# Row maxima turned by one product and a small DMA; half of head 1's mask moved from TensorE to VectorE

## The reference: two layers of attention, each with a feed-forward block behind it

```python
x = x + xattn0(layernorm(x), ctx, mask)       # 16 heads of 16; masked scores are -inf
x = x + moe_capacity(layernorm(x))            # top-2 of 8 experts, with a capacity
x = x + xattn1(layernorm(x), ctx, attn_mask)  # the same, but a float [512, 1024] mask is added to the scores
x = x + moe_top2(layernorm(x))                # top-2 of 8 experts
# attention: softmax over the 1024 keys of (q k^T / 4 + mask), times v, then a projection
```

## Time and profile before

| | |
|---|---|
| three runs | 1136.79, 1134.47, 1134.74 us; median 1134.74 |
| the profiled execution's own time | 1133.98 us |
| its span, first to last instruction | 1132.3 us |
| busy: TensorE, VectorE, ScalarE, GpSimd | 95%, 48%, 44%, 43% of the span |
| DMA | 170.52 MB, mean 151 GB/s |

### The profile page before, as it was taken

How to read it: one execution, slowest core, us unless ns; L and a number is a source line. 1 busy time by engine, 2 the same in 40 slices (tenths; PEclk the granted TensorE clock), 3 DMA queues, 4 the chain that set the end, 5 groups by cost and what they waited for, 6 DMA issues and landing times. The chain is left out here.

```text
span 1132.3 us, 25620 instructions
## 1 busy us (share of the span) xinstructions
PE 1078.0 (95%) x10259; PEld 770.2 (68%) x10259; DVE 547.0 (48%) x1534; ACT 493.4 (44%) x738; POOL 488.4 (43%) x510
## 2 busy tenths in 40 slices
PE   7899999999899999999899999999994999999997
PEld 4555655654578888888664344444454999999997
DVE  4579888864821111111347887777455122111221
ACT  4467777776531111111042788888853111111110
POOL 4457888883066892000004444444503223333232
PEclk8999999999999999999979999999998999999999
DMA  8744222002547964453079322210006999899970
GB/s 217 170 103 91 44 44 45 2 2 85 206 148 204 328 211 149 148 185 94 9 241 228 65 45 49 56 28 2 3 22 194 384 375 347 306 321 313 311 249 2
DMA packets 89632, 170.52 MB, mean 151 GB/s; under 512 B 11058, under 2 KB 61444, under 8 KB 87092
## 3 DMA queue, kind: packets, MB, share of 16 engines
q1 hardware_dynamic: 80916, 157.33, 44.4%
q0 software_dynamic: 6048, 8.28, 3.0%
q10 hardware_dynamic: 2560, 3.41, 1.1%
HBM read 150.19 MB, written 19.54 MB: 150 GB/s over the span
## 5 line engine op out<-in xcount | busy, mean ns | idle before, releaser
L189 PE MATMUL s_ps<-k_stack,q_stack 97*32 97x512 bf16 x1904 | 211.4, 382 | 2.8 <-ACT q_stack L281 2.3
L1488 ACT ACTIVATE prob<-st_ps 128x1024 f32<-128x1024 f32 x186 | 189.6, 1022 | 49.2 <-PE st_ps L189 44.8
L189 PE MATMUL st_ps<-q_stack,k_stack 100*32 100x512 bf16 x2048 | 193.2, 379 | 2.0 <-ACTq L1458 0.9
L252 DVE CUSTOM_DVE_ANT_0 junk<-s_ps,bias_rows,mx 128x512 f32<-128x512 f32 x240 | 170.1, 748 | 32.4 <-PE s_ps L189 32.4
L252 DVE CUSTOM_DVE_ANT_0 junk<-s_ps,bias_rows 128x512 f32<-128x512 f32 x236 | 154.6, 689 | 43.8 <-PE s_ps L189 43.7
L1935 PE MATMUL h_ps<-expert_in,w 128*128 (+1 forms) x704 | 153.5, 379 | 1.3 <-DMA w<-in_w 0.7
L1375 PE MATMUL o_ps<-prob,v_unit 128*32 128x512 f32 x1024 | 142.8, 595 | 4.3 <-POOL prob L1287 1.6
L1935 PEld LDWEIGHTS h_ps<-expert_in,w 128*128 128x128 f32 (+1 forms) x704 | 131.4, 187 | 22.0 <-issue 2.0
L1287 POOL TENSOR_TENSOR prob<-prob,keep_cols 128x1024 int32<-128x1024 int32 x56 | 132.9, 2383 | 21.4 <-ACT prob L1488 21.0
L2370 ACT ACTIVATE silu<-gu_ps 128x512 f32<-128x512 f32 x46 | 27.5, 597 | 227.3 <-PE gu_ps L2307 227.3
L189 PEld LDWEIGHTS st_ps<-q_stack,k_stack 100*32 100x32 bf16 x2048 | 72.6, 97 | 73.7 <-issue 21.0
(11 more groups left out here) (360 smaller groups left out, 1504.4 us busy)
## 6 DMA issues: line engine op xcount, KB each, us to landing
wg<-in_gateT SPq DMA_DIRECT2D x23, 1024.0 KB
wu<-in_upT SPq DMA_DIRECT2D x23, 1024.0 KB
wd<-in_downT SPq DMA_DIRECT2D x23, 1024.0 KB
w<-in_w SPq DMA_DIRECT2D x16, 1368.0 KB
w<-in_w SPq DMA_DIRECT2D x8, 1280.0 KB
k_stack<-k_scr SPq DMA_DIRECT2D x16, 384.0 KB, 5.1
k_stack<-k_scr SPq DMA_DIRECT2D x16, 256.0 KB, 5.5
k_scr<-k_parts SPq DMA_DIRECT2D x24, 128.0 KB, 2.7
```

The lines of the kernel that those rows point to most:

```text
L189: mm = pe.matmul(out[cols], weights[:, cols], moving, start=start, stop=stop)
L252: self.pr.nc.vector.tensor_tensor_reduce(out=self.junk[:, self.bank("job", u, j)], in0=self.ps[:, self.bank("job", u, j)], in1=self.m.bias ...
L1488: nc.scalar.activation(prob[:, n % 2, 2 * hp:2 * hp + 2], st_ps[:, 2 * hp:2 * hp + 2], ACT.Exp).then_inc(exp_done, 1)
```

## The change

**The turn** (both layers, all units but layer 1's unit 0). The parts are laid out part by part. One product of 128 rows, 24 columns (3 parts x 8 query blocks) and 128 moving columns against the identity writes [24, 128] to the bank. ScalarE copies it to `lines` in SBUF (`keep_lines`), and SP sends it with one DMA of 24 pieces of 256 bytes to the rows of the query stack (`send_lines`). `written` now waits for this DMA, and the ring's bank is free when ScalarE's copy is done.

**SP's order.** Its loop now runs over all units: the stacks of unit u + 3, after the same wait as before, then the two `send_lines` for unit u + 1.

**The mask of head 1** (layer 1, units 0 to 6, even steps). There is no product for head 1. VectorE adds the mask as it moves the scores from PSUM to `prob` (`second_mask`), behind the first job of the step, and `second_head` takes the exponential from there, behind a wait for `second_sum`. Odd steps are as before.

```diff
     def turn(self, pe, u, c2):
         pe.wait_ge(self.cut_done, (u - self.first) * 2 + c2 + 1)
         self.free(pe, "turn", u, c2)
+        if u == 0:
...
+        else:
+            mm = pe.matmul(self.ps[0:3 * 2 * QT, self.bank("turn", u, c2), 0:P],
+                           self.m.mpart[:, c2, 1:4].rearrange("p a q -> p (a q)"), self.pr.ident_bf[:],
+                           start=True, stop=True)
         mm.then_inc(self.turned, 1)
+
+    def keep_lines(self, act, u, c2):
+        act.wait_ge(self.turned, (u - self.first) * 2 + c2 + 1)
+        if u > 1:
+            act.wait_ge(self.rows_in[c2], 16 * (u - 1))
+        self.pr.nc.scalar.activation(self.lines[:, c2], self.ps[0:3 * 2 * QT, self.bank("turn", u, c2), 0:P],
+                                     ACT.Copy).then_inc(self.lines_out[c2], 1)
+
+    def send_lines(self, sp, u, c2):
+        i, b = divmod(u, B)
+        sp.wait_ge(self.lines_out[c2], u)
+        rows = self.pr.Q[b][MROW:ROWS, i % 2, 2 * c2:2 * c2 + 2]
+        sp.dma_start(rows.rearrange("a h (q n) -> a (h q) n", n=P), self.lines[:, c2]
+                     ).then_inc(self.rows_in[c2], 16)

     def written(self, pe, u, c2):
-        if u >= self.first:
-            pe.wait_ge(self.row_done, (u - self.first) * 2 + c2 + 1)
+        if u:
+            pe.wait_ge(self.rows_in[c2], 16 * u)
+        elif self.first == 0:
+            pe.wait_ge(self.row_done, c2 + 1)
...
-            return h < (1 if l == 1 and u < NU - 1 else 2)
+            return h < (1 if l == 1 and u < NU - 1 and kt % 2 else 2)
...
-                for u in range(2 * B, NU):
-
-                    sp.wait_ge(st_ready, (u - 3) * 16)
-                    passed(sp, sp_step)
-                    stacks(*divmod(u, B))
+                for u in range(NU - 1):
+
+                    if u >= 1 and u + 3 < NU:
+                        sp.wait_ge(st_ready, u * 16)
+                        passed(sp, sp_step)
+                        stacks(*divmod(u + 3, B))
+                    for c2 in range(2):
+                        row.send_lines(sp, u + 1, c2)
...
                 def second_head(n):
-                    act.wait_ge(st_ready, 2 * n + 1)
-                    nc.scalar.activation(prob[:, n % 2, 1], st_ps[:, 1], ACT.Exp).then_inc(exp_done, 1)
+                    if n % 2 == 0:
+                        act.wait_ge(second_sum, n // 2 + 1)
+                        src = prob[:, n % 2, 1]
+                    else:
+                        act.wait_ge(st_ready, 2 * n + 1)
+                        src = st_ps[:, 1]
+                    nc.scalar.activation(prob[:, n % 2, 1], src, ACT.Exp).then_inc(exp_done, 1)
...
+                def second_mask(u, kt):
+                    n = u * KT + kt
+                    dve.wait_ge(m.cols_in[kt // 4], 16)
+                    dve.wait_ge(st_ready, 2 * n + 1)
+                    dve.wait_ge(pv_done, n + 1)
+                    nc.vector.tensor_tensor(prob[:, n % 2, 1], st_ps[:, 1], m.cols[kt // 4][:, kt % 4],
+                                            ALU.add).then_inc(second_sum, 1)
+
                 for u in range(NU):
                     for kt in range(KT):
-                        row.maxima(dve, plan[u, kt])
+                        row.maxima(dve, plan[u, kt][:1])
+                        if l == 1 and u < NU - 1 and kt % 2 == 0:
+                            second_mask(u, kt)
+                        row.maxima(dve, plan[u, kt][1:])
```

More of the change, by code:

```diff
@@ L204, in __init__ @@
         self.turned, self.row_done = pr.sem(f"mt_done{l}"), pr.sem(f"mrow_done{l}")
+        self.lines = pr.sb(c, f"max_lines{l}", [3 * 2 * QT, 2, P], BF16)
+        self.lines_out = [pr.sem(f"lines_out{l}{i}") for i in range(2)]
+        self.rows_in = [pr.sem(f"max_rows_in{l}{i}") for i in range(2)]
         order = []
@@ L228, in free @@
                 pe.wait_ge(self.done, u * 32 + i + 1)
+            elif u == 0:
+                pe.wait_ge(self.row_done, i + 1)
             else:
-                pe.wait_ge(self.row_done, (u - self.first) * 2 + i + 1)
+                pe.wait_ge(self.lines_out[i], u)
     def scores(self, pe, jobs):
@@ L265, in cut @@
         if k >= 2:
-            pool.wait_ge(self.row_done, k - 1)
+            pool.wait_ge(self.turned, k - 1)
         split_max(self.pr, pool, self.m, b, c2, k, self.chain, self.cut_done)
@@ L271, in turn @@
         self.free(pe, "turn", u, c2)
-        out = self.ps[:, self.bank("turn", u, c2)].bitcast(BF16)
-        for q in range(2 * QT):
-            mm = pe.transpose(out[STACK:ROWS, q * P:(q + 1) * P], self.m.mpart[:, c2, q], self.pr.ident_bf[:])
-        mm.then_inc(self.turned, 1)
+        if u == 0:
+            out = self.ps[:, self.bank("turn", u, c2)].bitcast(BF16)
+            for q in range(2 * QT):
+                mm = pe.transpose(out[STACK:ROWS, q * P:(q + 1) * P], self.m.mpart[:, c2, :, q], self.pr.ident_bf[:])
+        else:
+            mm = pe.matmul(self.ps[0:3 * 2 * QT, self.bank("turn", u, c2), 0:P],
+                           self.m.mpart[:, c2, 1:4].rearrange("p a q -> p (a q)"), self.pr.ident_bf[:],
+                           start=True, stop=True)
+        mm.then_inc(self.turned, 1)
+    def keep_lines(self, act, u, c2):
[10 more added lines that the diff above has]
+                     ).then_inc(self.rows_in[c2], 16)
     def write(self, act, u, c2):
@@ L295, in split_max @@
     pool.wait_ge(chain, k * 4 + 1)
-    g.tensor_copy(m.mpart[:, c2, :, 1], m.mneg[:, c2]).then_inc(chain, 1)
+    g.tensor_copy(m.mpart[:, c2, 1], m.mneg[:, c2]).then_inc(chain, 1)
     pool.wait_ge(chain, k * 4 + 2)
-    g.tensor_tensor(m.mrest[:, c2], m.mneg[:, c2], m.mpart[:, c2, :, 1], ALU.subtract).then_inc(chain, 1)
+    g.tensor_tensor(m.mrest[:, c2], m.mneg[:, c2], m.mpart[:, c2, 1], ALU.subtract).then_inc(chain, 1)
     pool.wait_ge(chain, k * 4 + 3)
-    g.tensor_copy(m.mpart[:, c2, :, 2], m.mrest[:, c2]).then_inc(chain, 1)
+    g.tensor_copy(m.mpart[:, c2, 2], m.mrest[:, c2]).then_inc(chain, 1)
     pool.wait_ge(chain, k * 4 + 4)
-    g.tensor_tensor(m.mpart[:, c2, :, 3], m.mrest[:, c2], m.mpart[:, c2, :, 2], ALU.subtract).then_inc(cut_done, 1)
+    g.tensor_tensor(m.mpart[:, c2, 3], m.mrest[:, c2], m.mpart[:, c2, 2], ALU.subtract).then_inc(cut_done, 1)
 class FirstMax:
@@ L326, in turn @@
         for q in range(2 * QT):
-            mm = pe.transpose(self.ps[STACK:ROWS, q * P:(q + 1) * P], self.m.mpart[:, c2, q], self.pr.ident_bf[:])
+            mm = pe.transpose(self.ps[STACK:ROWS, q * P:(q + 1) * P], self.m.mpart[:, c2, :, q], self.pr.ident_bf[:])
         mm.then_inc(self.turned, 1)
@@ L1204, in attend @@
             m.cols_in = [pr.sem(f"cols1_in{i}") for i in range(2)]
-            raw_ready, raw_done, summed, first_exp = (pr.sem(x) for x in ("raw_ready", "raw_done", "summed", "first_exp"))
+            raw_ready, raw_done, summed, first_exp, second_sum = (
+                pr.sem(x) for x in ("raw_ready", "raw_done", "summed", "first_exp", "second_sum"))
             ask = Queries(pr, c, m, prob, row.ps, st_ps)
@@ L1529, in _ @@
                         if u + 1 < NU and kt in TURN_AT:
-                            row.write(act, u + 1, TURN_AT.index(kt))
+                            row.keep_lines(act, u + 1, TURN_AT.index(kt))
                 evacuate(NU - 1)
@@ L1676, in attention_memory @@
     m.mrest = pr.sb(c, f"mrest{l}", [P, 2, 2 * QT], F32)
-    m.mpart = pr.sb(c, f"mpart{l}", [P, 2, 2 * QT, 4], BF16)
+    m.mpart = pr.sb(c, f"mpart{l}", [P, 2, 4, 2 * QT], BF16)
     m.q_out = [[pr.sem(f"q_out{l}{i}{b}") for b in range(B)] for i in range(NG)]
```

## The result

The changed kernel takes 1125.76 us (median of 4 runs, 1125.34 to 1129.98), the kernel before 1135.68 beside it (4 runs, 1134.47 to 1136.79): ratio 0.9914, 95% interval 0.9893 to 0.9935, so 9.9 us faster. I predicted 1127.9, between 1122.0 and 1132.5. The profiled execution of after is the one of 1129.98: about 4 us of it were lost ahead of the first unit's end, where the granted clock was 0.50 (1.2 GHz) from 76 to 84 us and 1.00 in the trace of before. I compare stretches behind it.

What follows compares the result with a forecast made beforehand. TensorE was taken to bound both layers' loops. Terms 4.0 + 1.1 + 1.0 + 1.3 - 0.6 = 6.8 us took the profiled 1133.98 to 1127.2; with the median 0.76 above, 1127.9, range 1122.0 to 1132.5.

Steps and rivals of the forecast that it cites:

- The turn in layer 1: Layer 1, units 1 to 5: 0.22 us of TensorE and 0.20 of bank wait per turn, taken as 0.40; 4.0 in all.
- Unit 6: Layer 1's unit 6, where ScalarE becomes the bound: turns of steps 3 and 6 give 0.40 and 0.74, 1.1 us.
- rival 4: The turn's product empties the array and costs TensorE what the transposes did: gain only 3.2 us, 1131.5; chance 0.11.
- Layer 0: Layer 0's turns: `weigh` waits for GpSimd's `keep`, so the shorter turn saves only 1.0 us, between 0 and 3.1.
- The others about 0.1: Layer 0 turns other than step 3 where the values' bias is added: about 0.1 us each, 10 turns, 1.0.
- The masks: Layer 1 even steps, units 1 to 6: 0.22 us product saved, 0.16 stall of head 2, 0.06 left; 1.3 in all.
- rival 1: No stall from the masks, layer 0's turns count up to 3.1, unit 0 breaks even: gain 13.0 us, 1121.7; chance 0.17.
- rival 2: The masks take back what the turns give, unit 0 loses 2: gain 2.3 us, 1132.4; chance 0.13.
- Unit 0: Layer 1's unit 0, 44 jobs, VectorE nearly full: turns give 0.8 twice, masks cost more; a loss of 0.6 us.
- The DMA: Lines sent to the query stack: landing in 2.1 to 2.6 us, hidden in room of 3.3 (layer 1) and 3.6 (layer 0).

Runs made afterwards that it cites:

- e1: Changed kernel with the new turn only, head 1's mask made by TensorE in every step as before: 1124.59 us, ratio 0.9887.
- e4: Changed kernel with the turn's product issued eight times, each overwriting the last: one run, 1134.14 us.
- e5: Changed kernel with a ScalarE copy of 768 SBUF columns ahead of each short copy of the lines: one run, 1130.73 us.
- e6: Changed kernel with the lines sent, waited for and sent again, only the second landing told to TensorE: one run, 1127.86 us.
- e9: Changed kernel with four of the five instructions of GpSimd's maxima cut left out in layer 0 from the second unit's maxima on: one run, 1121.54 us.
- e11: Changed kernel with three early masks per unit (steps 0, 2, 4; units 1-6), layer 0's whole maxima cut on VectorE instead of GpSimd: 1165.16 us, ratio 1.0257.
- e12: Changed kernel with three early masks per unit (steps 0, 2, 4; units 1-6), first two of layer 0's five cut instructions on VectorE: 1125.03 us, ratio 0.9887.

## Why the prediction was right, step by step

**The turn in layer 1: right.** 0.40 per turn forecast, 0.85 / 2 = 0.43 by e1; its two parts (0.22 and 0.20) are the 0.21 and 0.20 of e1's steps, and e4 and e5 bring back one each. The copy was put at 0.28 and took 0.251. Unit 6: 1.1 forecast, 1.15 by e1 (the window of 22.6 us with ScalarE busy for 20.57, from which it was argued, is not among; from score to score it is 25.67 with 23.03), and the masks added 0.39 there where 0.12 was counted, most of it in steps 4 and 5 (5.84 against 6.11 in e1).

**The turn beside the array: rival 4 is out.** A product of 24 columns between products of 32 starts together with `weigh`, and e1's turn steps are at most 0.06 longer than others. The Trainium skill ("TensorEngine Tiling (Array Packing)", Key Properties) says that a change of tiling mode drains TensorE; these rows show no drain that could be measured, and whether 24 columns are another mode than 32 they don't show.

**Layer 0: mis-sized.** "The others about 0.1": I forecast 1.0 for the layer, it gave 2.33. Units with the values' bias gave 0.27 to 0.32 each, the others 0.53 to 0.56, and the last two of the seven 0.09 together. The mechanism was right, GpSimd's `keep` holds `weigh`, but only in after does it do so in full. The row of step 6 in the earlier trace rows is 1.24 long, where the same eight products take 1.07 when nothing is modelled before them; counted by its end, `weigh` began some 0.17 later than the 151.50 that I took, 0.40 behind `keep` and not 0.23. So 0.25 was free: from the end of `keep` to that of `weigh` step 6 has 1.46 in before and 1.22 in after, and in units without bias, where step 3 moves likewise, turn steps went from 3.49 to 3.21. I also read the rows of one kind of unit only.

**The masks: the stall right, the balance too good.** The add took 0.686 (0.69 forecast), head 2's stall is 0.17 (0.16), and a pair of steps takes 3.04 + 3.40 to 3.45, 6.44 to 6.49, against 3.19 + 3.25 = 6.44: the stall sits in the odd step, since head 2 is behind its first score. The sign that I had named for rival 1, an even step of 3.03, would have misled: the step takes 3.04, and only the pair shows the stall. What I left out is the turn: in steps 6 and 7 the mask behind the job makes the pair 6.64, against 6.56 in e1. So four masks give 0.09 per unit, not 0.24, and over the layer 0.14, not 1.3. Rival 1 is out (the stall is there), rival 2 nearly so: the masks do bring nothing, but don't take back what the turns give.

**Unit 0: wrong sign, small.** A loss of 0.6 was forecast, it gained 0.59. The turn gave 0.87 there by e1 (0.45 to 1.04 by all five executions without masks in it), and VectorE's 30.15 of 31.55 is the 30.2 that I had; what failed is "the masks cost up to 0.69 - 0.22 four times": with them and the new turn after, e6 and e9 take 31.96 to 32.04, which is within the 31.51 to 32.10 of those without. Unit 1 paid 0.3.

**The DMA: right that it is hidden**; the landing is 1.94, a little under the 2.1 to 2.6 that was taken, and the room 3.37 where 3.3 was.

In sum, turns 10 x 0.43 + 1.15 + 2.33 in place of 6.1, masks and unit 0 +0.14 and +0.87 in place of 1.3 and -0.6: 8.8 in place of 6.8. That the total came out so near is partly luck: the masks were put 1.2 too high and unit 0 1.5 too low, and the two errors nearly cancel; layer 0 is most of what is left.

## What to carry to other kernels

Eight small transposes in an engine's stream cost less than their own durations, but the PSUM bank that they hold and the long copy behind them cost as much again: count the turn as TensorE's time plus the bank's. Work moved from a full engine to a half-idle one is worth its step only if nobody waits for it at the new place; here one product less was 0.22, and 0.17 came back as the next head's wait. Where a ring of buffers fixes who waits for whom, try the moved instruction at each place in the order, by step, and leave it out of the steps whose ring place is taken.

## What the runs showed of the hardware

Small instructions of VectorE that began while GpSimd's mask product ran stood still until it ended. With two operands in SBUF (the subtractions of 128x8 in e11) 12 of 28 took 2.21 to 2.37 us and ended 0.02 to 0.03 behind the product; the other 16, begun with GpSimd idle or in the same moment as its product, took 0.17. With one operand (the negation, 128x8 f32) 12 of 14 in e11 and 12 of 14 in e12 took 0.26 to 1.03, and each ended 0.02 to 0.04 behind the product; the rest took 0.16 to 0.17. The casts of one operand took 0.17 everywhere, but that is no proof that they don't wait: none of the 14 of e12 lay beside a GpSimd instruction, and the five of e11 that overlapped one had begun before it. `second_mask`, with one operand in PSUM, took 0.684 to 0.691 beside GpSimd's adds.

The Trainium skill ("SBUF — State Buffer", SBUF: two separate sides) has this as a lock on a shared pair of ports, held for a whole instruction and taken on VectorE's side by one with two SBUF inputs (against a GpSimd instruction that reads SBUF) or by one in a two-port mode. The trace agrees for the subtractions, and the rule would have foretold e11; in which mode the negation ran no row shows. Small instructions don't escape it by being small.
